# The first layer norm, the first projections and the first maximum pass as one stage of a four-block attention kernel

## What is computed

```python
qkv = (_ln(x, g1, be1) @ w_qkv + b_qkv).reshape(b, t, 3, h, dh)   # 16 heads of 16
q, k_self, v_self = (qkv[:, :, 0], qkv[:, :, 1], qkv[:, :, 2])
ckv = (context @ w_ckv + b_ckv).reshape(b, s, 2, h, dh)
k = jnp.concatenate([k_self, k_ctx], axis=1); v = jnp.concatenate([v_self, v_ctx], axis=1)
scores = jnp.einsum('bthd,bshd->bhts', q, k) * scale
mask = (j >= t) | (j <= i)                                          # causal, context always seen
attn = jax.nn.softmax(jnp.where(mask, scores, -jnp.inf), axis=-1)
x = x + jnp.einsum('bhts,bshd->bthd', attn, v).reshape(b, t, d)
x = x + gelu(_ln(_ln(x, g2, be2), gf, bf) @ w1 + b1) @ w2 + b2
```

## Time and profile before

| | us |
|---|---|
| median of three runs | 1555.49 |
| profiled execution | 1554.63 |
| its span | 1552.9 |
| PE busy / DVE busy / ACT busy / POOL busy | 1338.1 / 1071.0 / 748.6 / 529.5 |
| start of norm, projections, first score product | 6.7, 25.4, 114.5 |

### The profile page before, as it was taken

One profiled execution on the slowest core, in us unless ns is written; L12 is line 12 of the kernel. 1 busy time (PEld: TensorE's weight loads), 2 busy tenths in 40 slices (PEclk: granted clock), 3 DMA queues, 4 the chain that ended last, 5 costly groups with the idle time before them and its releaser, 6 DMA issues.

```text
span 1552.9 us, 21719 instructions
## 1 busy us (share of the span) xinstructions
PE 1338.1 (86%) x7242; PEld 768.5 (49%) x7242; DVE 1071.0 (69%) x2669; ACT 748.6 (48%) x1046; POOL 529.5 (34%) x447
## 2 busy tenths in 40 slices
PE   5868999998789979889998979799998788788897
PEld 4513333332278756544443346443443677545796
DVE  4677888887654267766567777675767888676654
ACT  5405556666777345623334445233443734345664
POOL 3001111111330042306876622168865257001212
PEclk9959999999989999989999999799999889899998
DMA  7952333320000000554422306714400020730001
GB/s 256 260 126 47 59 58 62 66 47 2 28 0 1 1 1 34 157 176 96 96 50 46 115 35 196 195 38 95 96 28 1 28 35 22 164 65 3 1 1 54
DMA packets 79864, 110.29 MB, mean 71 GB/s; under 512 B 16591, under 2 KB 55689, under 8 KB 77961
## 3 DMA queue, kind: packets, MB, share of 16 engines
q1 hardware_dynamic: 79753, 108.91, 28.3%
HBM read 70.55 MB, written 37.80 MB: 70 GB/s over the span
## 4 chain that ended last, share of the span: by engine, by line
PE 40%; POOLq 19%; DVE 16%; issue 11%; ACT 7%; DVEq 3%; SPq 2%; DMA 1%; POOL 1%; ACTq 0%
POOLq L1109 18%; PE banks L1220 6%; PE banks L1565 5%; PE banks L1580 5%; PE banks L1162 4%; PE banks L1195 3%; PE banks L2151 3%; DVE mask_rows L1390 2%; PE banks L2181 2%; DVE max_parts L1394 2%; DVE scratch L1390 1%; PE banks L1173 1%; DVE max_parts L1379 1%; ACT x_feat L1355 1%; PE banks L2699 1%
## 5 line engine op out<-in xcount | busy, mean ns | idle before, releaser
L1355 ACT ACTIVATE x_feat<-banks,key_bias 128x1024 f32<-128x1024 f32 x160 | 176.4, 1115 | 264.6 <-PE banks L1202 208.7
L1108 POOL TENSOR_TENSOR x_feat<-x_feat 128x1024 f32<-128x1024 f32 (+1 forms) x112 | 243.0, 2169 | 97.0 <-ACT x_feat L1355 88.6
L1162 PE MATMUL banks<-stacks 128*128 128x512 f32 (+4 forms) x640 | 229.2, 406 | 36.5 <-DVE max_parts L1383 12.7
L1220 PE MATMUL banks<-x_feat,v_group 128*32 128x512 f32 (+4 forms) x1312 | 231.3, 568 | 8.4 <-ACT x_feat L1355 4.8
L1355 ACT ACTIVATE x_feat<-banks 128x1024 f32<-128x1024 f32 (+2 forms) x224 | 178.8, 841 | 111.7 <-PE banks L1195 110.5
L1162 PEld LDWEIGHTS banks<-stacks 96*128 96x128 bf16 (+1 forms) x640 | 78.5, 139 | 223.9 <-DVE max_parts L1383 91.6
L1132 POOL TENSOR_SCALAR_AFFINE_SELECT x_feat<-x_feat 128x256 f32<-128x256 f32 x128 | 53.7, 422 | 281.3 <-ACT x_feat L1355 279.6
L1195 PE MATMUL banks<-stacks 99*128 99x512 bf16 (+3 forms) x512 | 129.9, 344 | 20.1 <-ACT x_feat L1355 13.7
L1383 DVE CUSTOM_DVE_ANT_0 scratch<-banks,mask_rows 128x512 f32<-128x512 f32 x128 | 88.3, 689 | 50.6 <-PE banks L1162 50.4
L1201 PE MATMUL banks<-stacks 128*128 128x512 f32 x256 | 111.0, 434 | 9.5 <-DMA stacks<-neg_max_parts_r 9.5
L1565 PE MATMUL banks<-stacks 128*128 128x512 f32 x384 | 102.2, 405 | 9.3 <-DVE stacks L1547 8.4
(11 more groups left out here) (301 smaller groups left out, 2465.0 us busy)
## 6 DMA issues: line engine op xcount, KB each, us to landing
stacks<-q_parts_r SPq DMA_DIRECT2D x18, 512.0 KB, 11.9
stacks<-k_parts_r SPq DMA_DIRECT2D x18, 512.0 KB, 13.7
q_parts_r<-stacks SPq DMA_DIRECT2D x16, 512.0 KB, 3.2
k_parts_r<-stacks SPq DMA_DIRECT2D x16, 512.0 KB, 3.4
v_group<-v SPq DMA_DIRECT2D x14, 512.0 KB, 14.8
stacks<-q_parts SPq DMA_DIRECT2D x16, 384.0 KB, 5.0
w_even<-in_w SPq DMA_DIRECT2D x4, 1024.0 KB, 6.6
stacks<-q_parts SPq DMA_DIRECT2D x16, 256.0 KB, 5.4
```

The costliest lines, as they stand in the source:

```text
L1108: e.tensor_tensor(total, total, p, ALU.add)
L1162: m = e.matmul(PS[:, bank, at:at + wide], q[0:rows, h, qt * P:(qt + 1) * P], keys[0:rows, h, k0:k0 + wide], start=True, stop=True, skip_gr ...
L1220: m = e.matmul(PS[w * h:w * (h + 1), bank, t.q0:CH], V[:, h, :], PB[:, t.index % 2, h // 2, h % 2, 0:CH - t.q0], start=t.first, stop=t.las ...
L1355: e.activation(dst, PS[:, 2 * (st % 2):2 * (st % 2) + 2, 0:CH - t.q0], ACT.Exp, scale=A.scale, bias=bias).then_inc(s.p_ready, 1)
```

## The change

The stages norm and projection and the pass r = -1 of the first attention become one stage, "front", and every later stage number falls by one.

- Loads: `w_qkv`, `w_ckv` and the rows are issued behind chunk 1 of `x`, each with a semaphore of its own. `load_more` is issued in the attention, behind the stacks of group 2.
- Norm: VectorE, not ScalarE, makes the normalised tokens, into the place in `w_even` where `w1` goes later. Chunks 0 and 1 are made ahead of the items, chunk 2 and 3 at items number 6 to 16. The turns stand among the items too (`TURNS_AT`).
- Order: `[context item, q and k of chunks 0 and 1 for the first half of the features, the same for the second half, then chunk 2 and 3]`, so that group 0 needs only the first five feature items.
- Banks: features use three banks in place of four, values two in place of four, turns two, maxima two.
- The third part is GpSimd's. From pair 11 on each pair carries three chunks of the maximum pass, and remainders and values are made one pair later. The last 22 chunks follow the last pair.
- SP first issues 36 transfers that write the rows of ones of the three stacks from `ones_bf` (2 KB each), in place of GpSimd's fills; then the stores, and after ten items the q, k and context loads of group 0. Its value tiles, the stacks of group 1 and the three row transfers follow the last store, still in this stage.

```diff
+    FRONT_ROWS = WA[:, 2560:6656].rearrange("p (t d) -> p t d", d=D)
+    FRONT_SCR = [WA[:, 2560 + CH * i:2560 + CH * (i + 1)] for i in range(2)]
+    TURNS_AT = {0: [(0, 0), (0, 1)], 2: [(1, 0)], 4: [(1, 1)], 14: [(2, 0)], 16: [(2, 1)], 22: [(3, 0)], 24: [(3, 1)]}
+    STATISTICS_AT, NORMALISE_AT = {6: 2, 14: 3}, {8: 2, 16: 3}
+    MAXIMA_FROM, MAXIMA_EACH = 22, 3
...
+    def front_tensor(e, s, tn, tnc, nm, items, A):
+        turn_ctx_tensor(e, tnc, CTXN)
+        for number, (is_feature, it, i) in enumerate(in_order(items)):
+            for c, k in TURNS_AT.get(number, []):
+                n = KT * c + k
+                e.wait_ge(nm.normed, c + 1)
+                need(e, tn.taken, turn_needs(n))
...
+            if is_feature:
+                for x in front_maxima(A, i, 0):
+                    attention_chunk(e, A, *x, 0, -1)
+                need(e, s.left, i - 2)
...
+            else:
+                need(e, stored0.v_taken, i - 1)
...
+            for place in ((1,), (2,))[not is_feature]:
+                for x in front_maxima(A, i, place):
+                    attention_chunk(e, A, *x, 0, -1)
+        for x in front_maxima(A, len(items[0]), 0):
+            attention_chunk(e, A, *x, 0, -1)
...
+        def normalise_here(c):
+            scales(c)
+            e.drain()
+            for t in range(4 * c, 4 * c + 4):
+                z = e.tensor_scalar(FRONT_ROWS[:, t, :], X[:, t, :], RS[:, t:t + 1], NB[:, t:t + 1], ALU.mult, ALU.add)
+            z.then_inc(nm.normed, 1)
...
+            if is_feature:
+                maxima(i, 0)
+            for make, *of in late:
+                if make is (remainder if is_feature else value):
+                    make(*of)
+            late = [x for x in late if x[0] is not (remainder if is_feature else value)]
+            late.append((remainder if is_feature else value, it, i))
+            maxima(i, 2 - is_feature)
...
+    def front_gpsimd(e, s, items):
+        for i, it in enumerate(items[0]):
             e.wait_ge(s.second_part, i + 1)
             e.tensor_tensor(part(it, i, 2), RBUF[:, i % 2, 0:it.n], part(it, i, 1), ALU.subtract).then_inc(stored0.split, 1)
...
+    def ones_sync(e, A):
+        for u in range(A.slots):
+            k = slot16(A, u)[1]
+            for h in range(A.nh):
+                for row in range(K16, K16 + M_ROWS):
+                    e.dma_start(k[row:row + 1, h, P:P + T].rearrange("o (t n) -> o t n", n=P), ONEB[0:TB, :])\
+                        .then_inc(A.s.ones, 16)
+
+    def front_sync(e, items, A):
+        ones_sync(e, A)
+        for number, (is_feature, it, i) in enumerate(in_order(items)):
             store_item(e, is_feature, it, i)
+            if number == 2 * FIRST_FEATURES - 1:
+                e.wait_ge(A.s.cleared, 1)
+                for u in range(FIRST_FEATURES):
+                    e.wait_ge(part_stored[u], 16)
+                load_group(e, A, 0, 0, (0, 1, 2))
+        stored_after(e, len(items[0]), len(items[1]))
+        e.wait_ge(A.s.ones, 16 * A.slots * A.nh * M_ROWS)
+        load_group(e, A, 0, 0, (3,))
+        load_group(e, A, 1, 1)
+        send_maximum_rows(e, A, 0)
...
-                if A.self:
-                    fill(e, k[K16:K16 + M_ROWS, :, P:P + T], 1.0)
...
+    items0 = ([c0[0]] + pair(0, 0) + pair(1, 0) + [c0[1]] + pair(0, 1) + pair(1, 1) +
+              [x for c in (2, 3) for m in range(KT) for x in pair(c, m)],
+              [vc0[0]] + v0[0:4] + [vc0[1]] + v0[4:])
```

More of the change, by code:

```diff
@@ L63, in __init__ @@
         self.x_chunks = s[11:15]
+        self.w_ctx, self.rows0 = s[15:17]
 class NormSems:
@@ L108, in __init__ @@
         self.rows_sent = s[22:25]
-        self.triangle, self.second_summed = s[25:27]
+        self.triangle, self.second_summed, self.ones = s[25:28]
 class WindowSems:
@@ L298, in row @@
         return R[:, names.index(name), :]
[L301 removed]
+    ld = LoadSems(lasting("load", 17))
     query_stored = lasting("query_stored", 4)
@@ new lines, in turn_bank, with turn_needs @@
+    def turn_bank(n):
+        return PS[:, (3, 7)[n % 2] if n < 4 else 3, :]
+    def turn_needs(n):
+        return n - 1 if n < 4 else 3 if n == 4 else n
+    def front_tensor(e, s, tn, tnc, nm, items, A):
[5 more added lines that the diff above has]
+                need(e, tn.taken, turn_needs(n))
+                for j in range(4):
+                    m = e.transpose(turn_bank(n)[:, j * P:(j + 1) * P], FRONT_ROWS[:, 4 * c + j, k * P:(k + 1) * P], ID[:, :])
+                m.then_inc(tn.turned, 1)
+            if it.chunk is None:
+                e.wait_ge(tnc.taken, 1)
+                e.wait_ge(ld.w_ctx, 16)
+            else:
+                e.wait_ge(tn.taken, KT * (it.chunk + 1))
+                e.wait_ge(ld.w0, 16)
@@ new lines, in maxima @@
+        def maxima(pair, place):
+            for w, dg, k, n, bank in front_maxima(A, pair, place):
+                e.wait_ge(A.s.chunk_ready, n + 1)
+                if w in "AL":
+                    maximum_part(e, A, k, n, bank, 0, FRONT_SCR, w == "L")
+                else:
+                    maximum_split(e, A, 0, bank)
+        for c in range(2):
+            statistics(c)
+            if c > 0:
+                normalise_here(c - 1)
+        normalise_here(1)
+        e.wait_ge(ld.rows0, 16)
@@ new lines, in front_vector @@
+        late = []
+        for number, (is_feature, it, i) in enumerate(in_order(items)):
+            if number in STATISTICS_AT:
+                statistics(STATISTICS_AT[number])
+            if number in NORMALISE_AT:
+                normalise_here(NORMALISE_AT[number])
+            if number < MAXIMA_FROM:
+                (remainder if is_feature else value)(it, i)
+                continue
+            if is_feature:
[6 more added lines that the diff above has]
+            maxima(i, 2 - is_feature)
@@ L614, in third @@
+        for make, *of in late:
+            make(*of)
+        maxima(len(items[0]), 0)
+    def front_gpsimd(e, s, items):
+        for i, it in enumerate(items[0]):
             e.wait_ge(s.second_part, i + 1)
             e.tensor_tensor(part(it, i, 2), RBUF[:, i % 2, 0:it.n], part(it, i, 1), ALU.subtract).then_inc(stored0.split, 1)
-        last = None
-        for is_feature, it, i in in_order(sections):
-            if not is_feature:
-                value(it, i)
-                continue
-            e.wait_ge(s.first_part, i + 1)
-            need(e, stored0.split, i - 1)
-            e.scalar_tensor_tensor(RBUF[:, i % 2, 0:it.n], PS[:, i % 4, 0:it.n], it.bias, part(it, i, 0),
-                                   ALU.add, ALU.subtract).then_inc(s.left, 1)
-            if last is not None:
-                third(*last)
-            last = it, i
@@ L1008, in send_maximum_rows @@
             e.wait_ge(s.loaded[u + 2], low_loaded(A, g))
+        if A.self and A.dh == 16:
+            e.wait_ge(s.loaded[u + 3], 32 * (g // A.slots + 1))
         e.wait_ge(s.max_split, g + 1 + A.halved)
@@ L1045, in attention_sync @@
         lead = A.slots - 1 if A.self else 3
-        if A is at0:
-            for item in [*in_order(sections0)][-LAST_STORES:]:
-                store_item(e, *item)
-            stored_after(e, *items0)
         for g in range(1, first + 1):
-            load(g)
+            if A is not at0:
+                load(g)
         if A.halved and not A.first_in_front:
             send_first_rows(e, A, 0)
-        if not A.window and not A.halved:
+        if A is not at0 and not A.window and not A.halved:
             send_rows(0)
```

225 lines of the change are left out of this document (88 added, 137 removed).

## The result

The changed kernel takes 1550.16 us (median of 17 runs, 1544.73 to 1556.03) against 1558.3 (17 runs, 1551.62 to 1566.89): ratio 0.9949, 95% interval 0.9936 to 0.9962, so 8.1 us faster (6 to 10 by the interval). 16 us were forecast, and 1550.16 lies just outside the range of 1531 to 1550. The forecast of 1539.5 also started from a median of 1555.5, which is 1558.3 over more runs: of the 10.7 us between 1539.5 and 1550.2, 2.8 are that and 7.9 are gain that did not come. The profiled execution took 1551.2 us.

A forecast was written before the change was run, and what follows sets the result against it. Stages with different limits stand in a row: norm (ScalarE), projections (TensorE), first maximum pass (VectorE). 12.4 - 5.2 - 8.0 + 14.0 + 5.6 - 3.0 = 15.8, taken as 16 us: 1555.5 - 16 = 1539.5 us, range 1531 to 1550.

The forecast's parts named there:

- Start of the x projections: Norm made by VectorE: first x pair starts at 17.8 us where it started at 30.20, 12.4 us earlier.
- Pairs up to the eleventh: A context pair and three half turns cost 5.2 us; lead 7.2 us at pair 11, 46.2 us against 53.4.
- Pairs 11 to 17: Pairs with three maxima each, paced by TensorE: 26.0 us, costing 8.0, bringing 14.0 forward; 3 us friction added, from 0 to 9.
- The border and the tail: Behind the last product: 1.9 us replace 7.5, so 5.6 won; then the other 22 maxima take 15.7 us as before.
- SP's queue: 36 issues of ones at 0.5 us each: SP free at 24.7, stores can wait, cost nothing.
- (d): Rival: SP's queue becomes the bound at 1.27 us an issue, from about 1.15; 4 us lost, 1559.5; chance 0.06.
- The stacks of group 0: Loads behind the fifth feature item: 1.6 MB, 5.5 us at 300 GB/s, landed at 43, 3 us before pair 11.
- Rival (a): Stacks come late, everything stops at pair 11: at the bound 7.3 us more, 9 us won, 1546.5; chance 0.09.
- Last maximum to first score product: Last maximum, its split, three row transfers and their landing: 5.7 us, unchanged.
- Rival (b): Pairs don't overlap, so maxima and items add up: 8 us more, 9 us won, 1546.5; chance 0.08.
- (c): Rival: more than forecast, no friction and TensorE still at 2.4 GHz entering the attention; 21.5 us won, 1534; chance 0.07.
- (e): Rival: it does little, within 0.3%, by an SP issue of about 0.9 us or both (a) and (b); chance 0.06.

The follow-up runs named there:

- ones later: Changed kernel with the 36 transfers of ones issued three to a pair from pair 6 on, behind group 0's loads; ratio 0.994 to the kernel before.
- ones in the tail: Changed kernel without the 36 transfers; GpSimd fills the ones during the last 22 maxima; 1542.06 us, ratio 0.9911 to the kernel before.
- rows ahead: Kernel with ones filled in the tail, plus group 1's q, k and context loads issued before the stores land, its values behind the rows; 1542.94 us, ratio 0.9888.
- the first experiment: Changed kernel with the ones filled by GpSimd again as before and the 36 transfers gone; ratio 0.9967 to the kernel before.

## Why the prediction was partly wrong, by its steps

**Start of the x projections: right.** Forecast 17.8, measured 17.59, the normalising instruction 0.345 us against 0.304. That the instruction is so quick holds only because GpSimd no longer fills the ones beside it: I had called the fill's removal "nothing either way", and with the fill back the norm lost 5.6 us.

**Pairs up to the eleventh: right.** Pair 11 begins with its half turn at 45.47, forecast 46.2, and TensorE is ready for the stacks at 46.07. **Pairs 11 to 17: right in the sum, in part by luck.** They take 26.2 us (0.6 for the half turn ahead of the wait and 25.6 from its end to 81.1), 26.0 as summed and 29 with the friction of 3. The steady pairs take 3.2 to 3.3 us each, and no friction appeared; but the 26.2 contain the slow pair of 5.55 us, some 2 us of which are the lower clock, which was in no term. So the work itself was priced about 2 us too high (the self products at 0.25 where two take 0.60 and one 0.38, so 0.22 in a stream, are a small part of that), and the clock made it up. **The border and the tail**: 1.0 us instead of 1.9, and 15.8 against 15.7.

**SP's queue: the first step that failed, by size.** "I take 0.5, in the middle of 0.33 and 0.62": 36 issues took 26.06 us, 0.72 each, SP was free at 32.3 instead of 24.7, and the first load was issued at 42.41 instead of 35.2: **7.2 us**. I had written that this cost nothing, since stores can wait; but the loads stand in the same queue behind the stores. The kernels with ones later and in the tail issued the load at 36.94 and 36.23 and used it at 49.70 and 49.45, so 5.5 to 6.2 of the 7.2 are the queue's; the rest is that the fifth item and its landing come 1 to 1.7 us later than forecast. The price was not that of full DMA engines either, as I had feared in (d):

```profile
24.00:32.00 8.00, 7.81 (x27) 4.39 (x26) 7.39 (x20) 2.90 (x6) 3.47 (x3) 1.00 0.02 4
```
```profile
27.57 2.67 SPq L709 DMA_DIRECT2D stacks<-ones_bf  x4
```

With the DMA engines at a share of 0.02, four issues take 2.67 us, 0.67 each, above both ends of my bracket of 0.33 and 0.62. The late stores also stopped TensorE ahead of pair 11: without the ones in front it is ready at 44.9 to 45.4 (ones later, ones in the tail, rows ahead), with them at 46.1 to 48.3.

The Trainium skill ("DMA: Bandwidth & Descriptors", Rules for kernel authors) says that many small transfers should be joined. I let that count only for a rival, yet both remedies concerned them: to have no such transfers (load issued at 36.23) or to issue them behind the loads (36.94).

**The stacks of group 0: the step that failed worst.** "5.5 us at 300 GB/s": from first issue to use it is 13.1 us, not 7.8, **5.3 us** more. I had taken the rate of stretches in which large weight loads or stores ran; the nearest row for these very loads, 18.3 us from issue to use, was in my text as a bound and I explained it away by weights and values. Both together are 12.5 us; 3.1 us of slack lay ahead of pair 11, which leaves 9.4, and 9.48 were measured. Rival (a) is thus the mechanism that happened, beyond the bound that I had given it. Why the load takes 13 us is found only in part: by the estimate above its bytes are 7 to 8 and the context rows at most 1.0, and the other 4 to 5 stay open.

**Last maximum to first score product: off by 1.6.** "5.7, unchanged"; it is 7.3 (97.9 to 105.2), because group 1's load, issued at 88.33, is still in the engines; before, it was issued 26.7 us ahead of the rows (84.67 against 111.34), and now 12.0. This profile is at the mild end: it is 2.5 to 7.2 us from issue to use over the kernels, against 1.3 before. I had seen that the barrier moved and not what it had kept away from the rows.

The sum: 98.5 + 9.5 − 0.7 (pair 11's start) − 2.8 (pairs, 26.2 for 29) − 0.9 (border) + 0.1 (tail) + 1.6 = 105.3, measured 105.20. Two large errors of one sign, 7.2 and 5.3, were softened by the slack of 3.1 and by friction that did not come; that the total missed by only 7 us is in part luck. Rival (b) did not come about. Nor did (c): friction was nothing, but the clock in the first round is 0.50 (105.2 to 111.7) as before. Of (d) the mechanism acted, at 0.72 us an issue and not at its 1.15. And (e) was priced wrongly: by the working of (d), 0.9 us an issue leaves 9 to 10 us won and not nothing.

## What to carry to other kernels

When a stage is pulled forward, price its transfers from the row of the same transfer, issue to use, and not from bytes and a rate of other traffic: here 13.1 us against 7.8, and the order of one queue turned 7 us of issues that were called harmless into a wait of everything. Ask of each small transfer on the path (the rows of maxima) what large one was issued ahead of it; issued 15.8 us ahead it was out of their way, issued 10 to 12 us ahead it cost them 1 to 6 us. A wait of 5 us or more of TensorE is paid twice here, since the work behind it starts at the lower clock. And before one profile is compared with another, see how far profiles of the same work lie apart, here 2 us at pair 11.

## What the runs showed of the hardware that was not expected

VectorE's two-scalar instruction from SBUF to SBUF is held up as long as a GpSimd instruction runs beside it: one of 128x256 took 3.70 us beside a fill of 3.51 and ended 0.15 us behind it (the two lines in the first experiment), where four take 1.38 without a fill. Not every instruction is: the statistics (BATCH_NORM_STATS2, four in 1.40 us) took as long beside the fills as before. In the changed kernel the normalising of chunk 2 took 2.28 us beside GpSimd's subtraction, and 1.38 in the kernel where that is VectorE's and GpSimd idle; and one of 128x4 took 1.00 us, where it takes 0.17 alone:

```profile
26.59 1.16 POOL L682 TENSOR_TENSOR y_tok<-y_tok 128x512 bf16<-128x512 f32 x1 [1.42 <-ACT y_tok L587]
```
```profile
26.77 1.00 DVE L412 TENSOR_SCALAR var_eps<-mean_var 128x4 f32<-128x4 f32 x1
```

Reading PSUM, VectorE was not slowed by the same fills in the tail (from the last value product to the last transpose 19.04 us with them, 19.05 in the changed kernel). The Trainium skill ("SBUF — State Buffer", SBUF: two separate sides) describes this as a port pair that the two engines share and that one of them holds for a whole instruction; by that rule the fill belongs where VectorE reads PSUM, and the traces agree.

A 2 KB transfer of ones cost SP 0.72 us of its queue on average and 0.67 with idle DMA engines, more than an 8 KB row transfer (0.62) and more than a piece of the stacks of 384 KB (0.34 at 42.41).
